# Block inverse with coefficients and products in PSUM, segment sums with the constant triangle as weights, and new merge tables, in a one-core hybrid layer

## The reference

```
x = x + attn_a(ln(x))   # state-space layer, 8 heads, state 64
x = x + ffn(ln(x))      # ternary weights, 256 -> 1024 -> 1024 -> 1024 -> 256
x = x + attn_b(ln(x))   # delta rule, 8 heads of 32
x = x + ffn(ln(x))      # the same feed-forward weights
```

## Time and profile before

| | us |
|---|---|
| median of 3 runs | 2549.62 |
| their range | 2543.0 to 2551.01 |
| the profiled execution, device time | 2540.47 |
| its span in the profile | 2538.7 |
| PE busy in the span | 2285.3 (90%) |
| PE idle in the span | 253.4 |
| DVE, ACT, POOL busy | 1355.8, 1106.2, 844.6 |

### The profile page before, as it was taken

How to read it: one execution, slowest core, us unless ns; L and a number is a source line. 1 busy time by engine, 2 the same in 40 slices (tenths; PEclk the granted TensorE clock), 3 DMA queues, 4 the chain that set the end, 5 groups by cost and what they waited for, 6 DMA issues and landing times.

```text
span 2538.7 us, 61583 instructions
## 1 busy us (share of the span) xinstructions
PE 2285.3 (90%) x25057; PEld 2045.2 (81%) x25088; DVE 1355.8 (53%) x3346; ACT 1106.2 (44%) x2153; POOL 844.6 (33%) x1001
## 2 busy tenths in 40 slices
PE   5799986978998999988999989999899899999898
PEld 4688965867887888877888878878788787987788
DVE  4655154665545664465645566456563655546531
ACT  3465331643335633365333643347333473333233
POOL 3223331323333333333333333333333333333233
PEclk8799997988999999999999999999999999999999
DMA  8000000000100001000010000100010000000000
GB/s 253 1 1 1 1 18 18 2 1 18 30 7 1 2 19 33 4 1 2 18 35 2 1 5 16 35 2 2 8 31 17 1 1 18 22 7 18 18 10 9
DMA packets 85468, 43.84 MB, mean 17 GB/s; under 512 B 69936, under 2 KB 80048, under 8 KB 85168
## 3 DMA queue, kind: packets, MB, share of 16 engines
q1 hardware_dynamic: 81504, 28.11, 4.5%
q0 software_dynamic: 3664, 11.53, 1.4%
HBM read 27.05 MB, written 12.58 MB: 16 GB/s over the span
## 4 chain that ended last, share of the span: by engine, by line
PE 66%; DVE 15%; issue 7%; POOL 6%; ACT 4%; DMA 1%; SPq 0%; DVEq 0%; POOLq 0%; ACTq 0%
PE F L1317 29%; PE F L1297 6%; PE Q L1376 5%; PE F L1339 4%; POOL hA_lo L604 3%; PE Q L1477 2%; PE Q L1450 2%; PE Q L1433 2%; DVE hid L963 2%; PE Q L1545 2%; PE Q L1410 2%; PE Q L1388 1%; PE Q L1364 1%; PE Q L1557 1%; PE Q L1414 1%
## 5 line engine op out<-in xcount | busy, mean ns | idle before, releaser
L604 POOL TENSOR_TENSOR hA_lo<-hid,hA_hi 128x256 fp32r<-128x256 f32 (+1 forms) x384 | 361.4, 943 | 690.4 <-DVE hA_hi L967 346.4
L1317 PE MATMUL F<-hB_hi,h_sb 128*128 128x256 f32 x2048 | 512.1, 290 | 3.3 <-POOL hB_lo L604 2.7
L1317 PE MATMUL F<-hA_hi,h_sb 128*128 128x256 f32 x2048 | 509.6, 288 | 3.4 <-DVEq L966 2.4
L1317 PE MATMUL F<-hB_lo,h_sb 128*128 128x256 f32 x2048 | 499.1, 282 | 0.0
L1317 PE MATMUL F<-hA_lo,h_sb 128*128 128x256 f32 x2048 | 496.9, 282 | 0.0
L1317 PEld LDWEIGHTS F<-hB_hi,h_sb 128*128 128x128 f32 x2048 | 387.0, 189 | 14.2 <-POOL hB_lo L604 6.8
L1317 PEld LDWEIGHTS F<-hA_hi,h_sb 128*128 128x128 f32 x2048 | 386.1, 189 | 13.1 <-POOL hA_lo L604 5.2
L1317 PEld LDWEIGHTS F<-hB_lo,h_sb 128*128 128x128 f32 x2048 | 388.5, 190 | 0.0
L1317 PEld LDWEIGHTS F<-hA_lo,h_sb 128*128 128x128 f32 x2048 | 386.6, 189 | 0.3
L1297 PE MATMUL F<-xf_hi,w_sb 128*128 128x256 f32 x1024 | 282.8, 309 | 42.3 <-DVEq L966 32.6
L732 ACT ACTIVATE hid<-F,sh_sb 128x256 f32<-128x256 f32 x256 | 121.5, 475 | 425.4 <-PE F L1317 424.7
(11 more groups left out here) (198 smaller groups left out, 4124.6 us busy)
## 6 DMA issues: line engine op xcount, KB each, us to landing
h_sb<-h_dram POOLq DMA_DIRECT2D x2, 4096.0 KB, 23.9
x_sb<-x_dram SPq DMA_DIRECT2D x8, 512.0 KB, 4.2
a_scr<-amv SPq DMA_DIRECT2D x32, 128.0 KB, 2.3
au<-a_scr SPq DMA_DIRECT2D x8, 512.0 KB, 3.2
t_scr<-ti SPq DMA_DIRECT2D x8, 512.0 KB, 2.6
tbd<-t_scr SPq DMA_DIRECT2D x128, 32.0 KB, 1.9
out_dram<-x_sb SPq DMA_DIRECT2D x8, 512.0 KB, 3.0
w_sb<-w_dram POOLq DMA_DIRECT2D x3, 1024.0 KB, 7.9
```

What stands on the lines that cost most here:

```text
L604: pool.tensor_tensor(lo, hid[:, n % 2, 0:w, :], hi.bitcast(F32), ALU.subtract).then_inc(f_lo.handle, 1)
L1317: last = pe.matmul(ps[:, i * TOK:(i + 1) * TOK], w[:, k, o:o + P], part[:, k, :], start=(i == 0 and k == 0 and part is src[0]), stop=(i == ...
```

## The change

Three things change.

1. In the block inverse, ACT copies `au` from SBUF into two PSUM banks (Q0 and Q1) in two instructions of 512 elements, after the transfer has landed and the fourth tile's keys are done; DVE waits for that copy in place of the transfer, reads its coefficients from PSUM (`inv_au`) and writes its products into a third bank (`inv_prod`, Q2). `ti` stays in SBUF. `prod` in SBUF goes away.
2. DVE forms `seg` from `tri` in place of `stri`. PE has `stri` as the weights and four heads of `seg` (512 columns) as the moving matrix, so that a bank takes one matmul in place of four. The sums are the same.
3. All merge tables have other numbers. ACT's have one entry more in each delta stage, for the copy.

```
@@ -61,49 +61,49 @@
 BODY_PLAN = {
...
-    "act": ("1 2 0 0 2 2 0 1 0 0 0 1 21 1 2 3 4 4 0 4 3 0 1 3 0 0 0 2 0 2 0 0 1 0 0 0 0 1 1 0 0 1 0 0 1 0 0 "
...
+    "act": ("2 1 0 2 0 2 0 0 0 1 0 0 4 17 1 2 1 1 8 0 4 3 0 3 2 2 0 0 2 0 1 0 0 1 1 0 0 0 0 2 0 0 1 1 0 0 0 "
...
@@ -307,7 +307,6 @@
                 def s2_(name, shape):
                     return d2.enter_context(nc.sbuf_tensor(name, shape, F32))
                 au = s2_("au", [P, BLK, BLK])
-                prod = s2_("prod", [P, BLK * BLK // 4])
             with ExitStack() as d3:
                 def s3_(name, shape):
                     return d3.enter_context(nc.sbuf_tensor(name, shape, F32))
@@ -406,6 +405,7 @@
         d_pc = Signal(sem("d_pc"), NT)
         d_ast = Signal(sem("d_ast"), NT * 16)
         d_aun = Signal(sem("d_aun"), 16)
+        d_auc = Signal(sem("d_auc"), 1)
         d_inv = Signal(sem("d_inv"), 1)
         d_tst = Signal(sem("d_tst"), 16)
         d_tbd = Signal(sem("d_tbd"), NT * NB * 16)
@@ -433,6 +433,9 @@
         def uw_step(t):
 
             return D20 + D2_STEPS * (t - 1) + U_AHEAD if t else D20 - 2
+
+        inv_au = QB[:, 0:2, :].rearrange("p k (j i) -> p (k j) i", i=BLK)
+        inv_prod = Q[2]
 
         def walk_bank(t):
 
@@ -835,6 +838,12 @@
                         act.activation(sig[:], Q[1][:, 0:D + DH], ACT.Tanh, scale=0.5).then_inc(d_qkv.handle, 1)
                         act.copy(k_sb[:].rearrange("p h d -> p (h d)"), Q[0][:, D:2 * D])
                         act.copy(q_sb[:], Q[0][:, 0:D]).then_inc(d_q.handle, 1)
+                yield SUB0 - 0.5
+
+                act.wait_ge(d_aun.handle, d_aun.at(b, 16))
+                act.wait_ge(d_kn.handle, d_kn.at(b, NT))
+                act.copy(Q[0][:], au[:, 0:BLK // 2, :].rearrange("p j i -> p (j i)"))
+                act.copy(Q[1][:], au[:, BLK // 2:BLK, :].rearrange("p j i -> p (j i)")).then_inc(d_auc.handle, 1)
                 for t in range(NT + 1):
                     if t < NT:
                         yield uw_step(t)
@@ -1072,7 +1081,7 @@
                     if r < tiles:
                         yield SSM_STEPS * r + 6
                         dve.wait_ge(a_dta.handle, a_dta.at(b, r + 1))
-                        dve.tensor_tensor(seg[:], bcast(stri[:], 1, H), bcast(dta[:, r % 2, 1, :], 2, P),
+                        dve.tensor_tensor(seg[:], bcast(tri[:], 1, H), bcast(dta[:, r % 2, 1, :], 2, P),
                                           ALU.mult).then_inc(a_seg.handle, 1)
                         if (r + 1) % NT:
                             normed(xn[:], slots[r // NT], (r + 1) % NT, mv, rstd).then_inc(a_xn.handle, 1)
@@ -1156,12 +1165,12 @@
                     if j == 0:
                         dve.wait_ge(d_clear.handle, d_clear.at(b, 1))
                         dve.wait_ge(d_kr.handle, d_kr.at(b, NT))
-                        dve.wait_ge(d_aun.handle, d_aun.at(b, 16))
+                        dve.wait_ge(d_auc.handle, d_auc.at(b, 1))
                     below = BLK - 1 - j
-                    pr = prod[:, 0:(j + 1) * below].rearrange("p (c i) -> p c i", c=j + 1)
+                    pr = inv_prod[:, 0:(j + 1) * below].rearrange("p (c i) -> p c i", c=j + 1)
                     rest = ti[:, 0:j + 1, j + 1:BLK]
                     own(dve.tensor_tensor(pr, bcast(ti[:, 0:j + 1, j], 2, below),
-                                          bcast(au[:, j, j + 1:BLK], 1, j + 1), ALU.mult))
+                                          bcast(inv_au[:, j, j + 1:BLK], 1, j + 1), ALU.mult))
                     own(dve.tensor_tensor(rest, rest, pr, ALU.subtract))
                 dve.sem_inc(d_inv.handle, 1)
 
@@ -1423,15 +1432,11 @@
 
                         pe.wait_ge(a_seg.handle, a_seg.at(b, r + 1))
                         pe.wait_ge(a_zx.handle, a_zx.at(b, r + 1))
-                        for h in range(H):
-                            q = Q[1 + h // 4]
-                            if h % 4 == 0:
-
-                                pe.matmul(q[:], far_i[:], past[:].rearrange("p h t -> p (h t)"), start=True, stop=False,
-                                          skip_group_check=True)
-                            o = (h % 4) * P
-                            last = pe.matmul(q[:, o:o + P], seg[:, h, :], tri[:], start=False, stop=(h % 4 == 3),
-                                             skip_group_check=True)
+                        for i in range(2):
+                            pe.matmul(Q[1 + i], far_i[:], past[:].rearrange("p h t -> p (h t)"), start=True, stop=False,
+                                      skip_group_check=True)
+                            last = pe.matmul(Q[1 + i], stri[:], seg[:, 4 * i:4 * i + 4, :].rearrange("p h t -> p (h t)"),
+                                             start=False, stop=True, skip_group_check=True)
                         last.then_inc(a_segp.handle, 1)
                     if r:
                         yield SSM_STEPS * r + 7
```

30 lines of the change are left out of this document (17 added, 13 removed), and 70 rows, old and new, of tables (BODY_PLAN, FIRST_PLAN, LAST_PLAN, LATE_PLAN).

## The result

The changed kernel took 2566.4 us (median of 6 runs, 2551.62 to 2570.15) against 2550.32 us for the kernel before beside it (median of 6 runs): a ratio of 1.0060, 95% interval [1.0041, 1.0078]. The forecast was 2540 with a range to 2557: wrong in sign and outside the range.

What follows compares the result with a forecast made beforehand. PE bounds the kernel, busy 2285.3 of 2538.7 us. Segment sums -1, bodies -11, peeled +2.5, late +2.5, last -1, POOL's low parts about -1 make -9 us: forecast 2540 us, range 2522 to 2557.

Steps and rivals of the forecast that it cites:

- The inverse itself: Block inverse on DVE: operands in PSUM end the holding by POOL's reads, up to 5.9 us for each inverse.
- No surcharge for PSUM: DVE's inverse: PSUM operands cost the same as SBUF; rival: 65 ns on 62 instructions, 2544 us, chance 0.09.
- Segment sums, -1: Segment sums on PE, 32 tiles: fewer, longer matmuls save 0 to 1.6 us, taken as 1 us.
- worth on PE: 0: Inverse in the bodies: its chain gets shorter, but PE never waited for it, so 0 us.
- -11 for the table: New merge table in the bodies: shorter waits of PE, less new ones, -2.2 us each, -11 us for five.
- a rival (20 us, 0.16): Relief reaches the path: half of DVE's saved holding comes back as PE time, 20 us more, 2520; chance 0.16.
- 0, between -3 and +3: First window's table: two tiles' segment sums lose 2.4 and 1 us of FFN ahead, other steps gain as much: 0 us.
- The peeled window, +2.5: Peeled window: shorter inverse chain -1.8, moved FFN matmuls +5, fewer walk waits -0.7, net +2.5 us.
- The rival had +10: Peeled window in the slower case: long wait and lower clock through the walk, +10 us; case's chance 0.13.
- The late window, +2.5: Late window: nine walk steps stand bare in place of two, at 0.3 to 0.46 us, +2.5 us.
- The rival "slower": Whole kernel: peeled cover lost, low clock, bare late steps, bodies' gains eaten by new gaps: +12 us, 2562; chance 0.13.

Runs made afterwards that it cites:

- e5: Kernel before with both code edits (inverse in PSUM, segment sums turned round), old merge tables, ACT's copy placed early in the peeled window: ratio to before 0.9995.
- e3: Kernel before with the segment sums alone turned round: ratio to before 0.9992.
- e15: e7 with the segment sums as in the kernel before: ratio to before 0.9928.
- e7: Changed kernel with its new table in the five bodies alone, old tables elsewhere, early copy in the peeled window: ratio to before 0.9924, 2529.83 us.
- e6: Changed kernel with the first window's table alone put back to the old one: ratio to before 0.9977.
- e4: Changed kernel with the peeled window's table alone put back to the old one: ratio to before 1.0032.
- e9: Changed kernel with two FFN steps (32 matmuls) put back ahead of the peeled window's first `uw`, and two of ACT's with them: ratio to before 1.0037.
- e11: e7 with the new late table as well: ratio to before 0.9953.

## Why the prediction was wrong

*The inverse itself*: right. 21.2 us for each (about 21), none over 0.43 us (0.45), the wait at the end of the chain in the peeled window -2.1 us (-1.8, e5), the copies 0.58 us each (0.62).

*No surcharge for PSUM*: right, for the written operand too. The shortest product, 31 elements, takes 194 ns with a PSUM source and destination, and took 191 all in SBUF. By the 62 cycles of the Trainium skill (VectorE: DVE Perf Modes, section on the TRN2 errata) it would be 65 ns more; no run here shows them, and the measurement decides.

*Segment sums, -1*: right within what can be measured (e3: -1 us at equal clock, e15: 0).

*The bodies, "worth on PE: 0" for the inverse and -11 for the table*: the total was about right and put down to the wrong part. The length of five bodies fell by 10 us in the mean of the profiles and PE's idle time by 8 (the times at equal clock say 15, e7 against e3); the table alone brings 3 us of idle time and PSUM under it 5. Of the waits that I named, `hat` fell from 11.3 to 2.3 us in four bodies, `y` from 3.8 to none and the segment sums from 7.3 to 1.6, while `yT` (4.1 to 8.8 us) and the walk's `ur` (2.0 to 7.3) took back half of that. What PSUM adds is that the inverse is out of the way of DVE's evacuations. I had this as a rival (20 us, 0.16) and set it aside because no step of the inverse stood between the slices of the *old* order: the new order puts them there, and I did not look for it. In the changed kernel's own profile the gain does not show in the length (1517.6 us for the five bodies), but it does in PE's idle time: 21.4 us in a body where it was 22.5, with 20.6 forecast. e6, the same instruction for instruction from the peeled window on, has 1503.4 us. The one run had a mean clock of 0.953, the other 0.960, which is 241 and 203 us at the lower level ((1 - 0.953) x 2 x 2568 and (1 - 0.960) x 2 x 2540).

*The first window, "0, between -3 and +3"*: the step that failed first. I saw that tiles lose 2.4 us of FFN ahead of their segment sums, and wrote "other steps gain as much" without pricing one. FFN ahead of a step is worth its length as far as the step would wait without it, and nothing beyond. Three tiles lost 2.4 us each and stand 1.55 (the rest had been slack), 4.7 in all; first-layer slices wait 6.7 us more; the window grew by 12, and the table costs 17 in all.

*The peeled window, +2.5*: the wait was right (14.8 forecast, 15.45 measured), and so was its sign; the size was not. Its term for the moved matmuls was 5 us and they took 6.5, within the 3.8 to 6.8 given; what else moved in the walk, where the delay grows from 7.2 to 12.9 us, had no term. The rival had +10; 8.7 was measured (e4), half of it shown to be the two moved steps (e9). What makes the other half was not tested.

*The late window, +2.5*: 3 us by the mean of its windows, 7 by the time of e11. Its bare walk steps wait 0.48 us each for DVE's `ur` (0.46 counted); eight waits of first-layer slices for DVE, 4.7 us where there were 0.7, were not in the count.

*In sum*: the bodies gained about what was forecast. The forecast failed on the steps that it put at nothing or too low: 12 to 17 us for the first window in place of 0, 9 for the peeled one in place of 2.5, 3 to 7 for the late one in place of 2.5. The rival "slower" gave 2562 us, near the 2566 measured, but by another road: it had no cost in the first window and no gain in the bodies. That nearness is luck.

## To carry to other kernels

Ask of a reordering which steps wait in it that did not before: cover taken from a step costs its length less the slack that the step had, and no row of the old profile pays it back. Where an edit changes the length of work on one engine, judge it under the order that it comes with; a relief worth nothing in one order was worth 5 us of PE's waiting in another, 11 by the times. When a change comes as several tables for several stages, put each back alone: here one gained 15 us with the code and three lost 32, at equal clock. And set PE's idle time, window by window, beside the length: it repeated within 5 us where the length moved by 20.
